# A top-2 mixture of experts: from every expert on every token to routed blocks of 128 tokens

## The reference, cut to what matters

```python
def ffn(x, gate_w, gate_b, ew1, ew2, ew3, fc1, fc2, fc3):      # x: layernormed tokens
    probs = sigmoid(x @ gate_w.T + gate_b)                     # 6 experts
    w, idx = top_k(probs, 2)
    w = w / (sum(w) + 1e-08)
    ge = sum(one_hot(idx, 6) * w[..., None], axis=1)           # 0 for four experts of six
    for e in range(6):
        y += ge[:, e:e+1] * ((silu(x @ ew1[e].T) * (x @ ew3[e].T)) @ ew2[e].T)
    z = (silu(x @ fc1.T) * (x @ fc2.T)) @ fc3.T                # a shared expert
    return y + z
```

## Time and profile before

| | us |
|---|---|
| median of 3 runs | 1595.41 (1593.4 to 1597.21) |
| the profiled execution | 1592.61 |
| its span | 1590.8 |
| TensorE busy (matmul) | 1501.6, 94% of the span |
| VectorE busy | 967.9, 61% |
| ScalarE busy | 677.0, 43% |
| GpSimd busy | 286.2, 18% |

### The profile page before, as it was taken

How to read it: one execution, slowest core, us unless ns; L and a number is a source line. 1 busy time by engine, 2 the same in 40 slices (tenths; PEclk the granted TensorE clock), 3 DMA queues, 4 the chain that set the end, 5 groups by cost and what they waited for, 6 DMA issues and landing times.

```text
span 1590.8 us, 35333 instructions
## 1 busy us (share of the span) xinstructions
PE 1501.6 (94%) x12448; PEld 1360.0 (85%) x12448; DVE 967.9 (61%) x2720; ACT 677.0 (43%) x1430; POOL 286.2 (18%) x269
## 2 busy tenths in 40 slices
PE   5899999999876999999999999999999999999998
PEld 5798899889765888888888888887889999999998
DVE  5667656755653666666666666665566556656654
ACT  3434343434322555555555555555533332332332
POOL 2323322331233111111111121112220000000000
PEclk9999999999887999999999999999999999999999
DMA  7100000000023454454444444442200000000000
GB/s 172 41 1 0 0 0 0 0 0 0 19 56 105 119 118 117 114 122 113 115 115 114 112 112 112 114 112 69 71 26 1 12 12 0 12 12 0 12 12 13
DMA packets 73448, 89.58 MB, mean 56 GB/s; under 512 B 20480, under 2 KB 60928, under 8 KB 73392
## 3 DMA queue, kind: packets, MB, share of 16 engines
q1 hardware_dynamic: 72656, 88.52, 22.5%
q0 software_dynamic: 160, 0.23, 0.1%
q10 hardware_dynamic: 576, 0.07, 0.0%
HBM read 36.92 MB, written 3.67 MB: 26 GB/s over the span
## 4 chain that ended last, share of the span: by engine, by line
PE 81%; DVE 6%; issue 4%; ACT 2%; POOL 2%; SPq 1%; DMA 1%; DVEq 0%; ACTq 0%; POOLq 0%
PE psum L570 19%; PE psum L931 18%; PE psum L950 10%; PE psum L806 7%; PE psum L840 5%; PE psum L826 4%; PE psum L821 4%; PE psum L677 2%; PE psum L691 2%; PE psum L778 2%; PE psum L867 2%; PE psum L559 1%; PE psum L688 1%; SPq L365 1%; PE psum L853 1%
## 5 line engine op out<-in xcount | busy, mean ns | idle before, releaser
L1556 DVE CUSTOM_DVE_ANT_0 junk<-psum,biasq 112x375 f32<-112x375 f32 x512 | 260.5, 545 | 137.7 <-PE psum L806 102.3
L1202 ACT ACTIVATE pr<-psum 125x448 f32<-125x448 f32 x384 | 205.0, 544 | 127.5 <-PE psum L826 122.6
L826 PE MATMUL psum<-qst,kst 97*125 97x224 f32 x768 | 239.9, 352 | 0.0
L806 PE MATMUL psum<-kst,qst 96*112 96x376 f32 x512 | 177.5, 365 | 12.1 <-DVE smax L1556 10.2
L1309 ACT ACTIVATE sg<-psum 128x448 f32<-128x448 f32 x112 | 60.8, 545 | 249.5 <-PE psum L931 247.8
L826 PEld LDWEIGHTS psum<-qst,kst 97*125 97x125 f32 x768 | 145.9, 190 | 6.6
L821 PE MATMUL psum<-flagk,negbig 125*125 125x448 bf16 x384 | 139.0, 362 | 1.9 <-DMA qst<-negm 1.2
L931 PE MATMUL psum<-h3hi,ehi 128*128 128x448 f32 x448 | 135.1, 381 | 0.0
L1687 DVE TENSOR_TENSOR hid<-sg,psum 128x448 f32<-128x448 f32 x112 | 69.2, 620 | 107.1 <-PE psum L931 62.1
L931 PE MATMUL psum<-h3hi,elo 128*128 128x448 f32 x448 | 133.8, 377 | 0.0
L931 PE MATMUL psum<-h3lo,ehi 128*128 128x448 f32 x448 | 133.8, 378 | 0.0
(11 more groups left out here) (243 smaller groups left out, 3289.0 us busy)
## 6 DMA issues: line engine op xcount, KB each, us to landing
kst<-khi SPq DMA_DIRECT2D x64, 376.0 KB, 4.9
kst<-klo SPq DMA_DIRECT2D x32, 376.0 KB, 5.8
ctxT<-in_ctxT SPq DMA_DIRECT2D x32, 375.0 KB, 4.8
qst<-qhi SPq DMA_DIRECT2D x128, 56.0 KB, 1.9
stage<-in_e SPq DMA_DIRECT2D x21, 256.0 KB, 3.0
maskq<-in_mask SPq DMA_DIRECT2D x32, 164.1 KB
maskk<-in_maskT SPq DMA_DIRECT2D x32, 164.1 KB
x_res<-in_x SPq DMA_DIRECT2D x8, 448.0 KB, 11.5
```

The lines of the kernel that those rows point to most:

```text
L806: pe.matmul(bank[max_bank(n, hd)][0:T, 0:S2E], head(qst[par][0:ROWS], hd), pair(kst[par][0:ROWS], hd // 2), start=True, stop=True).then_in ...
L826: mm = pe.matmul(bank[q % 3][0:KP, cols(i, 2 * T)], pair(kst[par], n)[:, cols(q // HPB, KP)], both(qst[par], n), start=False, stop=True, s ...
L1202: nc.scalar.activation(pr[q % PROBS][:].rearrange("k i q -> k (i q)"), bank[q % 3][0:KP, 0:GT], ACT.Exp, scale=1.0 / HD ** 0.5).then_inc(s ...
L1556: nc.vector.tensor_tensor_reduce(out=junk[:, hd % 2, :], in0=bank[max_bank(n, hd)][0:T, 0:S2], in1=biasq[:, par, :], scale=1.0, scalar=-3e ...
```

## The change

The shared expert and the router are computed first, for all groups, in code written out eight times instead of a loop. Each group's tokens are given places: for every token and each of its two chosen experts, a row number in that expert's list. `places` does it with matmuls against a triangular matrix of ones (`earlier`), `slots` reads the row numbers out. GpSimd scatters the layernormed rows with 8 indirect DMAs per group (4 rows x 2 choices, 112 tokens of 1 KB) to `routed_h` in memory. When all counts are known, `plan_blocks` (some 20 small VectorE operations on one partition) works out for each of 64 block numbers the expert and the first row. Then 61 blocks of 128 list rows run in a software pipeline, two per turn of a `Fori`. The expert and the start row of a block are loaded from SBUF into a register (`value_load`): two such loads per block on TensorE, one on SyncE, one on GpSimd. SyncE loads the 128 rows, TensorE turns, expands (6 matmuls of 512 columns, with the tokens stationary and the weights of the two projections side by side as moving operand), turns the hidden values and contracts (6 matmuls of 256). GpSimd stores the 128 result rows to `routed_y` (128 KB), each store waiting until the one before has landed. Last, 64 indirect DMAs gather for each row of `x` the results of the first and of the second choice into six buffers, VectorE multiplies and adds each, and SyncE stores a group when its 8 are in.

Also added: at the start SyncE fills `routed_y` (22 MB) with zeros from SBUF. Weight pieces 3 to 20 are split three per group during the shared expert; three waits of `high_expert(0..2)` and one of GpSimd on the attention's buffers are gone, as the tiles lie elsewhere.

```diff
 @@ sync
+            for e in range(NE):
+                sp.dma_start(hbuf[e * CAP:e * CAP + BLK, :], zeros[:]).then_inc(s3["consts_in"], 16)
+                mine = ybuf[e * CAP:(e + 1) * CAP, :].rearrange("(p n) d -> p n d", p=P)
+                sp.dma_start(mine, zeros[:].unsqueeze(1).broadcast_to([P, CAP // P, D])).then_inc(s3["y_zeroed"], 16)
...
+            def block_pair(i):
+                for u in range(2):
+                    at = sp.value_load(start_i[0:1, bass.ds(i + u, 1)], min_val=0, max_val=NE * CAP - BLK)
+                    sp.wait_ge(s["h2t_ps"], 2 * G + i + u - 1)
+                    sp.dma_start(hblk[:, u], hbuf[bass.ds(at, BLK), :]).then_inc(s4[f"in{u}"], 16)
...
+            with sp.Fori(1, (NBLK + 1) // 2) as t:
+                block_pair(2 * t)
 @@ gpsimd
+            def scatter(g):
+                pool.wait_ge(s3["slot"], g + 1)
...
+                for j in range(GB):
+                    for r in range(TOP):
+                        to = bass.IndirectOffsetOnAxis(ap=slot[:, r, g * GB + j:g * GB + j + 1], axis=0)
+                        pool.indirect_dma_start(hbuf[:, :], to, h3[g % H3S][:, j, :], None).then_inc(s3[f"scat{g % H3S}"], 16)
...
+            for g in range(G):
+                for k in range(3):
+                    if 3 * g + k + 3 < 3 * (NE + 1):
+                        low_expert(3 * g + k + 3)
+                if g + 2 < G:
+                    rsqrt_group(g + 2)
+                scatter(g)
+            def store_block(i, u):
+                at = pool.value_load(start_i[0:1, bass.ds(i, 1)], min_val=0, max_val=NE * CAP - BLK)
+                pool.wait_ge(s4["y"], i + 1)
+                return pool.dma_start(ybuf[bass.ds(at, BLK), :], yb[:, u]).then_inc(s4[f"out{u}"], 16)
...
+            with pool.Fori(1, NBLK // 2) as t:
+                pool.wait_ge(s4["out1"], 16 * t)
+                store_block(2 * t, 0)
+                pool.wait_ge(s4["out0"], 16 * t + 16)
+                store_block(2 * t + 1, 1)
...
+                        if n >= YGS:
+                            pool.wait_ge(s3["x_new"], G + n - YGS + 1)
+                        of = bass.IndirectOffsetOnAxis(ap=slot[:, r, g * GB + j:g * GB + j + 1], axis=0)
+                        pool.indirect_dma_start(yg[n % YGS], None, ybuf[:, :], of).then_inc(s4[f"yg{n % YGS}"], 16)
 @@ tensor
+            def after_shared(g):
+                if g + 1 < G:
+                    transpose_group(g + 1)
+                if g > 0:
+                    contract(g - 1)
+                for w in range(2):
+                    if g + 1 < G:
+                        half_shared(g + 1, 0, w)
+                places(g)
+                for w in range(2):
+                    if g + 1 < G:
+                        half_shared(g + 1, 1, w)
...
+            def routed(turn, u, first=False, ahead=True):
+                i = 2 * turn + u
+                expand_block(i, u, block_of(i))
+                if not first:
+                    contract_block(i - 1, 1 - u, block_of(i - 1))
+                if ahead:
+                    transpose_block(i + 2, u, turn + 1)
+                transpose_hidden(i, u)
 @@ vector
+            for g in range(G):
+                hidden(g, 0)
+                low_hidden(g, 0)
+                hidden(g, 1)
+                add_gate_bias(g)
+                low_hidden(g, 1)
+                if g + 1 < G:
+                    low_h(g + 1)
+                gates(g)
+                if g > 0:
+                    accumulate(g - 1)
+                if g + 2 < G:
+                    group_moments(g + 2)
+                slots(g)
+                if g + 2 < G:
+                    normalise_group(g + 2)
+            plan_blocks()
+            accumulate(G - 1)
...
+            def routed(turn, u, first=False, ahead=True):
+                i = 2 * turn + u
+                hidden_block(i, u)
+                if u == 1:
+                    copy_y(turn, 0)
+                elif not first:
+                    copy_y(turn - 1, 1)
                 if ahead:
+                    low_block(i + 2, u)
+                low_hidden_block(i, u)
```

More of the change, by code:

```diff
@@ L46 @@
 NE, EW = 6, 256
+TOP = 2
+BLK = 128
+CAP = B * T
+NBLK = (TOP * B * T + NE * (BLK - 1)) // BLK
+AHEAD = 64
+H3S = 4
+YGS = 6
+U32 = mybir.dt.uint32
 GB = 4
@@ L925, in half_expert @@
                 if it >= 2:
[L926 to L929, removed]
+                    pe.wait_ge(s[left], SHARED + it - 1)
+                parts = [(half_weight(wp, w, c, m), hp[:, c]) for wp, hp in ((0, h3hi), (1, h3hi), (0, h3lo)) for c in range(DC)]
@@ L956, in transpose_group @@
                     pe.wait_ge(s3["logit"], g)
[L957 to L968, removed]
+                if g >= 2:
+                    pe.wait_ge(s3["slot"], g - 1)
@@ new lines, in routed, with routed_blocks @@
+            def routed(turn, u, first=False, ahead=True):
[6 more added lines that the diff above has]
+                transpose_hidden(i, u)
+            def routed_blocks():
+                pe.wait_ge(s4["plan"], 1)
+                pe.wait_ge(s3["x_new"], G)
+                for u in range(2):
+                    transpose_block(u, u, 0)
+                for turn in range(2):
+                    for u in range(2):
+                        routed(turn, u, first=turn == 0 and u == 0)
+                with pe.Fori(2, NBLK // 2) as t:
+                    for u in range(2):
+                        routed(t, u)
+                routed(NBLK // 2, 0, ahead=False)
+                contract_block(NBLK - 1, 0, block_of(NBLK - 1))
@@ new lines, in _ @@
+            with dve.Fori(2, NBLK // 2) as t:
+                for u in range(2):
+                    routed(t, u)
+            routed(NBLK // 2, 0, ahead=False)
+            copy_y(NBLK // 2, 0)
+            for g in range(G):
+                for r in range(TOP):
+                    for j in range(GB):
+                        n = (g * TOP + r) * GB + j
+                        dve.wait_ge(s4[f"yg{n % YGS}"], 16 * (n // YGS + 1))
+                        if r == 1:
+                            dve.wait_ge(s3["x_new"], G + n - GB + 1)
+                        row = x[:, g * GB + j]
+                        nc.vector.scalar_tensor_tensor(out=row, in0=yg[n % YGS], scalar=gate[:, r, g * GB + j:g * GB + j + 1], in1=row, op0=ALU.mult, op1=ALU.add).then_inc(s3["x_new"], 1)
```

566 lines of the change are left out of this document (382 added, 184 removed).

## The result

The changed kernel takes 1626.8 us against 1594.5: ratio 1.0193, interval 1.0174 to 1.0212. It is slower by 1.9%, where 1573 and a gain of 1.4% were forecast. Its profiled execution spans 1625.6 us, 56.6 more than the forecast's sum of 1569.

What follows compares the result with a forecast made beforehand. TensorE's columns were taken to bound the experts. From the attention's end at 1123.2, phase 1 ran to 1244, blocks from 1261 to 1475, gathers and output to 1559, plus 10 for first passes: 1569, stated as 1573, range 1500 to 1670.

Steps and rivals of the forecast that it cites:

- Phase 1: Shared expert for eight groups: VectorE's work and waits set 15.8 us a group, last row numbers at 1244 us.
- The 10 us for first passes: Code written out eight times has more first passes: three stretches of 4.77 us, 10 net, between -5 and +25.
- Phase 2: The loop over 61 blocks: two coupled chains of equal length give 3.5 us a block, 214 us in all.
- rival C: Loop over blocks: a register load costs 1.8 us, both chains go to 4.6, total 1640; chance 0.13.
- TensorE's period: Loop over blocks: expand, wait for hidden values, register load and dynamic addresses take TensorE 3.4 us a block.
- The store chain: Loop over blocks, GpSimd: each store waits for the landing before, then loads its register: 3.4 us a block.
- Between the phases: From the last row numbers to the first block's expand: last scatters, landing, first load and transposes, 1244 to 1261 us.
- D: Rival for the loop over blocks: TensorE's clock drops to 1.2 GHz, period some 5.9 us, total 1719; chance 0.05.
- A: Rival: queues run ahead, blocks take 2.8 us and an indirect issue 0.75, total about 1505; chance 0.20.
- The price c: An indirect DMA's cost on GpSimd, in scatters and gathers: 1.15 us, twice the direct issue.
- B: Rival for the final gathers and the scatters: an indirect DMA costs GpSimd 2.0 us, total 1666; chance 0.22.
- The sign: Whole kernel: faster by 22 us (1.4%); chances faster 0.55, same 0.04, slower 0.41.

Runs made afterwards that it cites:

- e3_splits: The changed kernel with GpSimd's three weight splits of a group waiting until VectorE is through with the gates: 1608.8 us, ratio 1.0075 to the kernel before.
- e5_halfrows: The changed kernel with each gather fetching 56 rows and not 112: 1629.5 us, a single run.
- e8_all_loads: The changed kernel with TensorE's loop written out, register loads ahead of waits on TensorE and GpSimd, and weight splits behind the gates: 1552.1 us, ratio 0.9728.

## Why the prediction was wrong, step by step

- **Phase 1, 15.8 us a group: wrong, 20.** The sum of VectorE's work and waits was near: e3_splits, which only takes the hold away, has 15.9 to 16.5. (Its terms as written add up to some 15.3 and not 15.8: 12.9 of work and 2.4 of waits.) The step that failed is the overlap, "ScalarE ... and GpSimd lie beside it": VectorE stood still for 3.3 to 4.2 us in each of six groups while GpSimd split. That is 19 of the 30 us, by the row numbers in e3_splits. The other 11 are in e3_splits too: groups up to 0.7 longer than the sum, and the first group's waits for TensorE (2.72 and 3.33), which the sum did not have. I compared GpSimd's length with the group's and didn't ask whether the two engines can run at once. It was in the rows: the earlier trace rows shows 4.77 us of waiting for nothing, and I called it a first pass through code. The trace of before from 1157 us on, VectorE and GpSimd:

```profile
1158.17 7.86 DVE L1692 TENSOR_TENSOR hid3lo<-hid,hid3hi 128x448 fp32r<-128x448 f32 x2
```
```profile
1157.46 7.55 POOL L546 TENSOR_TENSOR elo<-stage,ehi 128x512 fp32r<-128x512 f32 x6
```

  Two subtractions of 0.62 take 7.86 while GpSimd splits six times, and the operation has two SBUF inputs. Before the change the splits were over with the first group, and the holds cost that group alone (this one, and three comparisons of 0.82, 1.27 and 1.27 at 1133 to 1136). The change put three splits into the gates of each of six groups.
- **The 10 us for first passes: wrong**, for the same reason. The 4.77 that they were priced by was a hold.
- **Phase 2, 3.5 us a block: wrong, 3.90.** The register load was priced well (0.6 against 0.5), and rival C (1.8) fell. The 600 ns that the prediction quotes from the Trainium skill (DMA: Bandwidth & Descriptors, Latency and other measured facts) as a floor of a tensor_load is above what the trace has: 0.30 for the load itself. The step that failed is TensorE's period, 1.40 + 1.03 + 0.05 + 0.9 = 3.38, measured 3.94 in the turn shown. Two terms were short. From expand to hidden transposes 2.66 and 2.76 passed for 2.43, since silu began 1.77 after the expand: the last matmul's tail and the first handoff are longer than I took them. From the transposes to the next expand 1.04 and 1.42 passed for 0.95; the sum had no branch, and the branch with its steps is the 0.38 between the two. I also charged one load where two stand in the queue; as the kernel is, the second costs little, about 0.1 in every second block, since it runs beside the expand. (The 0.3 for dynamic addresses had no row; the queue steps between load and expand took 0.34.) The store chain, forecast at 3.4, is 3.34, though its parts were off both ways (landing 2.0 for 2.7); it did not bind, as TensorE's was longer.
- **Between the phases, 17 us: right** (17.3), and the loop's clock stayed at 1.00: D fell. A fell: a load does not run ahead of a wait that stands before it (blocks at 3.90, not 2.8), and an indirect issue costs 1.24, not 0.75.
- **The price c: 1.24 for 1.15, right in size, wrong in kind.** I took twice the direct issue for a pass over the rows, and e5_halfrows shows no cost per row, so the near hit is luck. The gathers' 64 issues cost 5 us more than forecast. B's price of 2.0 did not come; its place, a tail with GpSimd alone, was in the sum too and is 79 us.
- **The attention's end: 5 us late**, within what executions differ by.
- **The sign**: the 22 us of forecast gain were smaller than either miss, 30 in phase 1 or 27 in the loop. Either alone would have used them up.

The routing itself was not at fault: e8_all_loads, which computes the same with the same tiles, is 2.7% faster than the kernel before.

## What to carry to other kernels

Before calling two engines parallel, look in the trace for an instruction of one that is many times its usual length and ends with an instruction of the other; here steps of VectorE of 0.16 us took 1.2 to 4.4 beside GpSimd's splits. In a loop with dynamic addresses, count what each queue does between a wait and the next (loads, branch), put the loads ahead of the wait, and work out every chain of the loop, since shortening one of two near-equal chains gives little, and both a lot (8 us and about 0 alone, 41 together). An indirect DMA cost GpSimd the same for 56 rows as for 112 (0.92 and 0.93): have few, and have them beside other work.

## What the runs showed of the hardware

- An indirect DMA of 112 rows of 1 KB held GpSimd for 0.93 to 0.94 us with a gap of 0.30, scatter or gather; a gather of 56 rows for 0.92. It landed after 2.5 (scatter) and 2.7 (gather).
- A register load took 0.30 us on TensorE's queue (0.5 with what follows), the loop's branch 0.21.
- A store of 128 KB issued by GpSimd landed after 2.0 us. The prediction quotes the fit of the Trainium skill (DMA: Bandwidth & Descriptors, Anatomy of one DMA), which gives 2.3; the measured time is 0.3 shorter.
- Small VectorE operations of 0.16 us took 1.2 to 1.3 beside one split of GpSimd, and up to 4.38 beside three back to back; adds with one operand in PSUM and moments kept their 0.41 beside the same splits.
- TensorE's clock fell to 1.2 GHz after an idle time of 1.22 us, while ten small matmuls ran (0.80 from 1206 to 1208, then 0.50); the idle time of the earlier trace rows was 2.51. In the loop, with pauses of 0.6 to 1.0 between matmuls, it stayed at 2.4 GHz (1.00 from 1300 to 1500).
